# Two transformer layers on one core: every piece at another place of its round and in another PSUM bank

## The reference

```python
    x = x + _layernorm(_L0_attn_ref(_layernorm(x, axis=-1), L0_attn_Wq, L0_attn_bq, L0_attn_Wk, L0_attn_bk, L0_attn_Wv, L0_attn_bv, L0_attn_Wo, L0_attn_bo), axis=-1)
    x = x + _layernorm(_L0_ffn_ref(_layernorm(x, axis=-1), L0_ffn_w_gate, L0_ffn_w_up, L0_ffn_w_down), axis=-1)
    x = x + _layernorm(_L1_attn_ref(_layernorm(x, axis=-1), L1_attn_Wq, L1_attn_Wk, L1_attn_Wv, L1_attn_Wo), axis=-1)
    x = x + _layernorm(_L1_ffn_ref(_layernorm(x, axis=-1), L1_ffn_W_r, L1_ffn_W_k, L1_ffn_W_v, L1_ffn_mu_r, L1_ffn_mu_k), axis=-1)
    return x
```

```python
            xr = mu_r * x + (1.0 - mu_r) * x_prev
            xk = mu_k * x + (1.0 - mu_k) * x_prev
            r = jax.nn.sigmoid(jnp.einsum('btc,dc->btd', xr, W_r))
            k = jnp.einsum('btc,dc->btd', xk, W_k)
            k_act = jnp.square(jax.nn.relu(k))
            out = r * jnp.einsum('btc,dc->btd', k_act, W_v)
```

## Time and profile before

| | |
|---|---|
| median of three runs | 1496.42 us (1495.2 to 1499.88) |
| the profiled execution | 1490.64 us, span 1488.8 |
| PE busy | 1402.8 us (94%), 12438 matmuls |
| DVE busy | 1082.9 us (73%) |
| ACT busy | 800.0 us (54%) |
| POOL busy | 788.5 us (53%) |
| mean granted clock of TensorE | 0.994 |
| a looped round of layer 0 (318.84 to 395.97, same wait in each) | 77.13 us |
| a looped round of layer 1 (1071.18 to 1173.74, same wait in each) | 102.56 us |

### The profile page before, as it was taken

One profiled execution on the slowest core, in us unless ns is written; L12 is line 12 of the kernel. 1 busy time (PEld: TensorE's weight loads), 2 busy tenths in 40 slices (PEclk: granted clock), 3 DMA queues, 4 the chain that ended last, 5 costly groups with the idle time before them and its releaser, 6 DMA issues. The chain is left out here.

```text
span 1488.8 us, 32925 instructions
## 1 busy us (share of the span) xinstructions
PE 1402.8 (94%) x12438; PEld 1042.0 (70%) x12438; DVE 1082.9 (73%) x2067; ACT 800.0 (54%) x1135; POOL 788.5 (53%) x994
## 2 busy tenths in 40 slices
PE   5889999999999998999999999999999999999996
PEld 4566767676767675777777777767677677677775
DVE  7888888888888877755567585585685665765766
ACT  2555444444444445555766656656556666566652
POOL 4344434444444442444666575666575565766652
PEclk8999999999999999999999999999999999999999
DMA  5221212112020122100100000010100100100001
GB/s 182 83 86 48 72 58 73 58 58 70 36 78 25 67 80 100 43 29 29 65 2 1 15 29 2 1 44 1 43 1 1 43 1 1 43 1 30 2 1 43
DMA packets 36547, 61.40 MB, mean 41 GB/s; under 512 B 3760, under 2 KB 19024, under 8 KB 36432
## 3 DMA queue, kind: packets, MB, share of 16 engines
q1 hardware_dynamic: 35568, 59.09, 11.4%
q10 hardware_dynamic: 864, 0.66, 0.2%
HBM read 25.86 MB, written 8.42 MB: 23 GB/s over the span
## 5 line engine op out<-in xcount | busy, mean ns | idle before, releaser
L1740 ACT ACTIVATE l_probs<-psum 128x1024 f32<-128x1024 f32 (+1 forms) x192 | 164.5, 879 | 165.2 <-PE psum L2074 127.8
L929 ACT ACTIVATE l_probs<-psum 128x512 f32<-128x512 f32 x256 | 138.3, 593 | 175.2 <-PE psum L1195 165.8
L321 POOL TENSOR_SCALAR_AFFINE_SELECT l_probs<-l_probs 128x256 f32<-128x256 f32 (+1 forms) x384 | 179.4, 498 | 0.0
L1012 DVE TENSOR_REDUCE l_rowmax<-psum 128x2 f32<-128x1024 f32 (+2 forms) x192 | 158.9, 862 | 20.4 <-PE psum L1156 19.8
L1836 DVE TENSOR_TENSOR l_qk_lo<-psum,l_qk_hi 128x1024 fp32r<-128x1024 f32 x64 | 77.6, 1218 | 117.0 <-ACT l_qk_hi L1730 116.5
L2117 PE MATMUL psum<-l_probs,l_v 128*32 128x512 f32 (+3 forms) x2048 | 151.8, 434 | 11.6 <-DVE l_qk_lo L1836 9.8
L1746 ACT ACTIVATE l_probs<-l_probs 128x2048 f32<-128x2048 f32 (+1 forms) x128 | 160.4, 1274 | 1.3
L1845 DVE RECIPROCAL l_keysum<-psum 128x256 f32<-128x256 f32 x64 | 112.3, 1754 | 44.0 <-PE psum L2103 37.4
L2117 PEld LDWEIGHTS psum<-l_probs,l_v 128*32 128x32 f32 x2048 | 65.5, 110 | 92.8 <-issue 80.2
L316 POOL TENSOR_TENSOR l_pool_holder<-expo 128x1 f32<-128x1 f32 x128 | 26.2, 204 | 195.5 <-ACT l_probs L1746 130.0
L1858 DVE TENSOR_TENSOR l_att<-psum,l_keysum 64x256 f32<-64x256 f32 x256 | 107.8, 421 | 15.9 <-PE psum L2117 9.1
(11 more groups left out here) (240 smaller groups left out, 4134.8 us busy)
## 6 DMA issues: line engine op xcount, KB each, us to landing
l_kT<-l_roped_hi SPq DMA_DIRECT2D x32, 256.0 KB, 2.7
l_qT<-l_roped_hi SPq DMA_DIRECT2D x32, 256.0 KB, 2.5
x_mid<-l_x SPq DMA_DIRECT2D x8, 516.0 KB, 2.7
l_x<-x_mid SPq DMA_DIRECT2D x8, 516.0 KB, 3.3
l_xin<-in_x SPq DMA_DIRECT2D x8, 512.0 KB, 4.0
l_kT<-l_roped_lo SPq DMA_DIRECT2D x16, 256.0 KB, 2.8
l_qT<-l_roped_lo SPq DMA_DIRECT2D x16, 256.0 KB, 2.4
l_x<-in_x SPq DMA_DIRECT2D x8, 512.0 KB, 4.1
```

The costliest lines, as they stand in the source:

```text
L321: nc.gpsimd.affine_select(out=part, in_=part, compare_op=ALU.is_ge, fill=0.0, base=0, pattern=[[0, part.shape[1]], [1, P]], channel_multip ...
L929: space.free(nc.scalar.activation(probs[:, SLOT[p], e, c0:c1], space.unit(*use), ACT.Exp, scale=HD0 ** -0.5), *use)
L1012: reduced = nc.vector.tensor_reduce(rowmax[:, a // 2, :, a % 2, t], space.unit("max", a, k)[:, :, c0:c0 + (t + 1) * P], mybir.AxisListType ...
L1740: space.free(nc.scalar.activation(probs[:, p % 2, :, c0:c1], space.unit("score", p, u)[:, :, 0:c1 - c0], ACT.Tanh, scale=HD1 ** -0.5 / CLA ...
```

## The change

No operation is added or removed, and SLOTS, LOOP and all code around the tables stay. The numbers of nine tables change: of each layer the table of places, the moved_table of the first and last rounds and the bank_table, for layer 0 also the loading_table, for layer 1 also the one that places its weight loads, and with them the order of the pieces on each engine, in the loop and outside, and the banks. A few of the lines:

```diff
     table = {
...
-        "x_norm": {(): -16.219},
+        "x_norm": {(): -17.22},
...
-        "load_lo": {(4,): -55.741, (5,): -55.738, (6,): -55.735, (7,): -54.344, (8,): -44.553, (9,): -20.93, (10,): -15.315, (11,): -13.174, (12,): 2.905, (13,): 16.717, (14,): 18.636, (15,): 21.12},
+        "load_lo": {(4,): -48.117, (5,): -43.669, (6,): -43.644, (7,): -43.585, (8,): -42.071, (9,): -42.036, (10,): -36.121, (11,): -4.092, (12,): -3.633, (13,): 12.19, (14,): 23.508, (15,): 23.51},
...
-        "x4_rstd": {(): 52.383},
+        "x4_rstd": {(): 48.712},
-        "x4_norm": {(): 51.224},
+        "x4_norm": {(): 52.099},
...
-        "load": {(0,): 203.592, (1,): 170.206, (2,): 193.357, (3,): 170.207, (4,): 263.379, (5,): 261.668, (6,): 281.294, (7,): 279.261, (8,): 298.223, (9,): 289.222},
+        "load": {(0,): 207.906, (1,): 209.887, (2,): 209.112, (3,): 184.872, (4,): 217.484, (5,): 216.238, (6,): 279.702, (7,): 285.768, (8,): 288.712, (9,): 291.156},
```

More of the change, by code:

```diff
@@ L577, in phase1 @@
-        "o": {(0,): 35.756, (1,): 36.093},
-        "o_out": {(0,): 35.764, (1,): 37.091},
-        "x1_T": {(0,): 41.314, (1,): 41.689},
-        "x1_T_hi": {(0,): 42.55, (1,): 43.21},
-        "x1_T_lo": {(0,): 42.737, (1,): 42.763},
-        "o_stats": {(): 37.454},
-        "o_rstd": {(): 34.318},
-        "residual": {(): 40.842},
-        "o_norm": {(): 38.909},
-        "x1_stats": {(): 38.916},
-        "x1_rstd": {(): 37.241},
-        "x1_norm": {(): 41.386},
-        "gate": {(0,): 42.773, (1,): 44, (2,): 46.261, (3,): 46.36, (4,): 46.461, (5,): 51.676},
@@ L604, in phase1 @@
[L604 to L605 removed]
+        "load_x": {(): -15.319},
+        "x_stats": {(): -18.194},
+        "x_rstd": {(): -22.344},
+        "x_norm": {(): -17.22},
+        "x_T": {(0,): -13.659, (1,): -12.596},
+        "x_T_hi": {(0,): -9.127, (1,): -9.12},
+        "x_T_lo": {(0,): -12.303, (1,): -12.14},
+        "rope": {(0,): -7.674, (1,): -4.98, (2,): 0.001, (3,): 4},
@@ new lines, in phase1 @@
+        "outT": {(0,): 20.514, (1,): 25.407, (2,): 33.004, (3,): 33.469},
+        "outT_norm": {(0,): 17.861, (1,): 25.659, (2,): 32.378, (3,): 34.108},
+        "att_T": {(0,): 33.924, (1,): 34.008},
+        "att_T_hi": {(0,): 38.134, (1,): 38.644},
+        "att_T_lo": {(0,): 34.408, (1,): 34.909},
+        "o": {(0,): 35.441, (1,): 36},
+        "o_out": {(0,): 36.205, (1,): 36.727},
+        "x1_T": {(0,): 41.867, (1,): 41.994},
+        "x1_T_hi": {(0,): 43.2, (1,): 43.334},
+        "x1_T_lo": {(0,): 40.501, (1,): 41.818},
@@ new lines, in phase1 @@
+        "o_stats": {(): 37.091},
+        "o_rstd": {(): 36.857},
+        "residual": {(): 42.459},
+        "o_norm": {(): 37.818},
+        "x1_stats": {(): 38.26},
+        "x1_rstd": {(): 39.429},
+        "x1_norm": {(): 39.636},
+        "gate": {(0,): 44.145, (1,): 44.8, (2,): 48.256, (3,): 49.306, (4,): 50.214, (5,): 51.733},
+        "tanh": {(0,): 44.75, (1,): 49.549, (2,): 52.277, (3,): 52.616, (4,): 55.616, (5,): 56.388},
+        "gated": {(0,): 41.858, (1,): 44.211, (2,): 48.237, (3,): 49.537, (4,): 50.909, (5,): 52.507},
```

449 lines of the change are left out of this document (219 added, 230 removed), and 9 rows, old and new, of the table moved_table.

## The result

The changed kernel takes 1456.17 us (median; 1455.32 to 1456.88), the kernel before, run beside it, 1495.81. The ratio is 0.9734, with an interval of 0.9708 to 0.9761: 39.6 us less. The forecast was 1476. The profiled execution took 1455.32 with a span of 1453.6, 35.2 less than the 1488.8 of before.

What follows compares the result with a forecast made beforehand. PE's waits, one by one, were taken as the bound, with 86.0 us idle in the first block. Terms -11.7 - 4.8 - 4 + 0 + 0 = -20.5 from 1496.4 gave 1475.9; range 1463 to 1491.

Steps and rivals of the forecast that it cites:

- Layer 1, looped rounds: Four rounds of layer 1: 3.93 us of PE waits go, 1.0 comes back, net 2.9 a round, -11.7 in all.
- The three waits: Layer 1 rounds: PE waits of 2.46 at pv(0), 0.45 at pair 2's key sums, 1.02 at the key product, all gone.
- the one at qk(2): Layer 1 rounds: new PE wait for banks att(7) frees behind x4_norm, 0.5 to 3.9 us possible, 0.7 taken.
- The 0.3 for x3_T: Layer 1 rounds: 0.3 us added for the transpose of x3, which now follows att(1) and x3_norm closely.
- Rival 1: Layer 1: POOL beside x4_norm keeps it slow, qk(2) waits 3.9 us, layer 1 gives nothing: 1488.7; chance 0.17.
- Rival 2: Layer 1: late rstd blocks DVE at x4_norm, holding recip(7), att(7) and qk(2); 1507.5 at 7.9 us delay; chance 0.06.
- Rival 3: Whole kernel: new PE waits of 0.2 to 0.7 us could come back 30 times, leaving 1496; chance 0.12.
- Layer 0, looped rounds: Four rounds of layer 0: x_norm moved behind rmax removes a 1.20 us wait; net -1.2 a round, -4.8.
- Between the layers: Layer change: SP's new order removes the 4.76 us row-maxima wait and its clock loss, 6.6; 2.6 set against it, net -4.
- First rounds and end: First rounds, paced by DVE: 0, bounds -6 and +6; end of the kernel: 0, bounds -3 and +3.
- with PE busy as now: Sign for the window 0 to 50 us: PE's busy time there stays as before, 33.5 us.
- The carry-over: Whole kernel: the median's 5.8 us above the profiled execution, not in the trace, is kept in the forecast.

Runs made afterwards that it cites:

- three: Kernel before with x4_rstd, x_rstd (GpSimd) and x_norm (VectorE) moved in layer 1's looped rounds, TensorE's order kept: 1477.56 us, ratio 0.9877.
- x4_early: Kernel before with x4_stats, x4_rstd and x4_norm moved earlier in layer 1's looped rounds, nothing else: 1510.82 us, ratio 1.0109.
- heat_bank: Kernel before with layer 0's dummy pieces heat(0), heat(2), heat(4) moved to PSUM bank 3: 1505.92 us, ratio 1.006.
- fill0: Kernel before with TensorE's rope(0) and max(5,1) moved ahead of dummies and score products in layer 0's looped rounds: 1497.13 us, ratio 1.0015.
- maxima_all: Kernel before with the residual and all four layer 1 weight loads behind the first two row-maxima transfers on SP's queue: 1498.46 us, ratio 1.0015.

## Why the forecast was wrong, step by step

**Layer 1, looped rounds: right in mechanism, -11.7 against -18.9.** The three waits were worth their size (three), and the one at qk(2) was 0.45 where 0.7 was taken, from a chain that was worked out well (8.9 us forecast, 8.5 measured). What failed is the list: it took 3.93 of 4.91 us of idle time. The other four waits, 0.19 to 0.32 us each, had no term; of them only 0.19 at pv(3) is left, and 0.19 at qk(2) is part of the 0.45. And the busy time fell from 97.65 to 96.82, 0.8 us a round that no term had; three shows that part of this comes with the waits themselves. The 0.3 for x3_T did not come. Of the 2.1 us a round that the forecast missed, 0.8 are the small waits, 0.8 the busy time, and some 0.5 new waits that were taken too large.

**Rival 1 (x4_norm stays slow)**: false for this place (1.38 for four, below the 1.62 taken as the low bound), true 14 us earlier in the round (4.47). The reading of POOL's order decided it rightly. **Rival 2 (a blocked DVE)** did not happen with the rstd, but its price is shown by x4_early: with DVE's new place and PE's old order the kernel is 17 us slower. The rstd late in the new order itself was not tried. **Rival 3 (waits only move)** is false in layer 1, and nearly true for every single move in layer 0 and between the layers.

**Layer 0, looped rounds: -4.8 against -8.0, mechanism half wrong.** x_norm was forecast at 1.20 a round and gave 0.56. The three waits of 0.6 to 0.7 us were put down to the chain from the output product to the gate; their rows name exponentials and a mask, heat_bank and fill0 show that it is these that are waited for, and the forecast took them as nearly fixed (1.98 to 1.7) where the new order halved them.

**Between the layers: -4 against -5.1, right size, cause shown in part only.** The wait and the low clock behind it are gone from the changed kernel, as forecast. But SP's order, to which the forecast gave both, is not enough: maxima_all removes the wait and gains nothing. The step that failed is "what is late next": it was asked of DVE and x1_T, and not of the exponentials. That the size came out is partly luck.

**First rounds and end: 0 against -2.3, -1.1 and +0.3**, within their bounds. PE's busy time in the first 50 us fell to 29.7 from 33.5 and the mean clock to 0.86 from 0.90, against the sign "with PE busy as now". At pv(0) of batch 1 the changed kernel was still behind (110.50 against 109.24), and the lead stands only from about 205 us on.

**The carry-over: 4.9 us.** The forecast added to the profiled span the 5.8 us by which the median lay above the profiled time. It was no constant. The 83 executions of the kernel before that ran beside the experiments go from 1491.1 to 1502.8, in step with their mean granted clock: the fourteen at 0.993 took 1491.9 in the mean, the seven at 0.985 took 1500.0. So one execution spends more time at half clock than the next; where, only profiled ones show. The changed kernel, with few long waits, ran from 1455.3 to 1456.9 in four executions, and its median is 0.9 above its profiled time. 14.8 us of the miss are in the profiled execution, 4.9 here.

**The range**: its low end, 1463, was put at about 31 us less, "and not all at once". 31 less is 1465, and not all at once would be more. The measured time lies below either.

## What to carry to other kernels

Follow a wait to the end of its chain and move the one instruction that is late, not the piece that stands in front: one rstd of 1.0 us moved alone gave 12 us, 9.9 of them in the four rounds, while the piece behind it moved with its neighbours lost 17. Ask of each wait what is late next on every engine, since a wait that covers another is worth little; rounds that repeat tell it to 0.05 us where totals can't. And count the small waits: of a round that stands 4.9 us in seven waits, a new order may take nearly all.
